# Normalised input moved from MID to H, squares in a four-slot buffer, and a new order of the token tiles in one feed-forward stage

## The reference

```python
xc = jnp.concatenate([o1, o2], axis=-1) @ up_w + up_b     # (2048, 512) @ (512, 1024)
x = residual + xc                                         # residual = xn
h = rmsnorm(x, norm2_w)                                   # x * rsqrt(mean(x*x) + 1e-6) * w
ffn = jax.nn.gelu(h @ ffn_w1 + ffn_b1, approximate=False) @ ffn_w2 + ffn_b2
return x + ffn                                            # hidden size 2048
```

## Time and profile before

| | us |
|---|---|
| median of 2 runs | 2920.51 (2918.38 to 2922.63) |
| profiled execution, its own time | 2919.8 |
| span of its slowest core (core 2) | 2918.3 |
| spans of the eight cores | 2908.5 to 2918.3 |
| TensorE busy, of the span | 2542.4 (87%) |
| VectorE busy, ScalarE busy | 559.1 (19%), 627.8 (22%) |

### The profile page before, as it was taken

The page is one execution under the profiler, slowest core; times in us unless marked ns, Lnnn a source line. Parts: engine busy times, 40 slices in busy tenths (PEclk is TensorE's granted clock), DMA queues, the critical chain, the costliest instruction groups (busy, mean ns, idle before and its releaser), DMA issues.

```text
span 2918.3 us, 30150 instructions; the slowest of 8 cores (2908.5 to 2918.3 us)
## 1 busy us (share of the span) xinstructions
PE 2542.4 (87%) x11144; PEld 1120.6 (38%) x11344; DVE 559.1 (19%) x699; ACT 627.8 (22%) x966; POOL 61.6 (2%) x80
## 2 busy tenths in 40 slices
PE   3865665666896978999999999999999999999999
PEld 1322332332332433444444444444444444444443
DVE  5115743643214000010011001001100100100000
ACT  2332232330111211112211211221121122112222
POOL 0000000000000010000000000000000000000000
PEclk9986555556896989999999999999999999999999
DMA  6020000007000047007007007007006105203011
GB/s 148 15 46 1 1 1 1 1 1 116 1 0 1 1 62 112 1 1 116 1 1 116 1 1 116 0 1 102 14 1 90 26 1 74 42 1 58 33 41 44
DMA packets 65621, 100.92 MB, mean 35 GB/s; under 512 B 4819, under 2 KB 40148, under 8 KB 65484
## 3 DMA queue, kind: packets, MB, share of 16 engines
q0 software_dynamic: 58080, 80.78, 19.1%
q1 hardware_dynamic: 7404, 18.20, 1.9%
HBM read 171.36 MB, written 8.39 MB: 62 GB/s over the span
## 4 chain that ended last, share of the span: by engine, by line
PE 85%; issue 7%; DVE 4%; DMA 2%; ACT 2%; SPq 0%; another core or an unknown queue 0%; POOL 0%; DVEq 0%; ACTq 0%; POOLq 0%
PE PF L1119 31%; PE PF L1100 29%; PE PF L1008 4%; PE PF L983 4%; PE PBF L682 3%; PE PF L697 3%; PE PF L381 2%; DMA WE<-e2w 1%; PE PBF L925 1%; PE PF L639 1%; PE PF L556 1%; PE PBF L341 1%; DVE H L972 1%; DMA c_qb<-qb 1%; PE PF L712 1%
## 5 line engine op out<-in xcount | busy, mean ns | idle before, releaser
L1119 PE MATMUL PF<-WE,EHS 128*128 128x512 bf16 x4016 | 913.5, 380 | 34.1 <-DMA WE<-e2w 10.0
L1100 PE MATMUL PF<-XN,WE 128*128 128x512 bf16 x4012 | 887.3, 380 | 19.1 <-DMA WE<-e1w 14.7
L1107 ACT ACTIVATE EHS<-PF,c_eb1c 128x512 bf16<-128x512 f32 x512 | 352.2, 688 | 1348.1 <-PE PF L1100 1346.0
L1119 PEld LDWEIGHTS PF<-WE,EHS 128*128 128x128 bf16 x4096 | 390.5, 98 | 544.8 <-issue 100.9
L1100 PEld LDWEIGHTS PF<-XN,WE 128*128 128x128 bf16 x4096 | 401.3, 98 | 499.8 <-issue 20.4
L1137 DVE SCALAR_TENSOR_TENSOR S<-PF,WTM,S 128x1024 bf16<-128x1024 f32 x128 | 164.3, 1284 | 1688.5 <-PE PF L1119 1469.5
L682 PE MATMUL PBF<-c_idb,E 120*120 120x120 bf16 (+1 forms) x288 | 91.2, 317 | 52.7 <-DVE E L676 15.1
L983 PE MATMUL PF<-H,WF 128*128 128x512 bf16 x502 | 119.2, 399 | 8.0 <-ACT MID L990 7.0
L1008 PE MATMUL PF<-WF,MID 128*128 128x512 bf16 x500 | 115.4, 380 | 4.6 <-ACT MID L990 3.9
L697 PE MATMUL PF<-PTS,VT 120*32 120x120 bf16 x272 | 70.9, 261 | 36.5 <-ACT UPIN L722 1.1
L682 PEld LDWEIGHTS PBF<-c_idb,E 120*120 120x120 bf16 (+1 forms) x288 | 48.8, 169 | 92.9 <-issue 90.7
(11 more groups left out here) (129 smaller groups left out, 970.7 us busy)
## 6 DMA issues: line engine op xcount, KB each, us to landing
WE<-e1w POOLq DMA_DIRECT2D x32, 1024.0 KB, 41.4
WE<-e2w POOLq DMA_DIRECT2D x32, 1024.0 KB, 20.7
XST<-x SPq DMA_DIRECT2D x16, 512.0 KB, 3.4
out<-OST SPq DMA_DIRECT2D x16, 512.0 KB, 2.6
WF<-f1w POOLq DMA_DIRECT2D x1, 4096.0 KB, 29.1
WF<-f2w POOLq DMA_DIRECT2D x1, 4096.0 KB, 53.9
WR<-r1w POOLq DMA_DIRECT2D x1, 2048.0 KB, 31.5
WDOWN<-dw POOLq DMA_DIRECT2D x1, 1024.0 KB, 18.8
```

Source lines behind the costliest of these rows:

```text
L1100: (lambda m=m, nt=nt, k=k, ps=ps, slot=slot: t_.matmul(ps[:, 0:512], WE13[slot][:, k, 128 * m: 128 * m + 128], XN3[:, k, 512 * nt: 512 * n ...
L1107: P.op("scalar", (lambda e=e, m=m, ps=ps: s_.activation(EHS3[:, m, 0:512], ps[:, 0:512], AF.Silu, bias=CS["eb1c"][:, 16 * e + m: 16 * e + ...
L1119: lambda k=k, h2=h2, tcl=tcl, e=e, PEx=PEx: t_.matmul(PEx[0:128, 512 * h2: 512 * h2 + 512], EHS3[:, k, 128 * tcl: 128 * tcl + 128], WE23[: ...
```

## The change

`XA` moves from the two halves of `MID` into the half of `H` that the tile's normalised values will take, so `a4_h` works in place, and `XA`'s resource is that half's. Squares go to the first 2048 columns of `MID`, which hold four of them: `a4_sq` now records four squares, their four statistics matmuls, four squares, four matmuls, and `a4_stats` keeps only Ln and Exp. The order by hand is new: tiles 0 and 1 pass one after the other through up, transposes, squares and statistics; of tile 2, up and transposes stand before the second feed-forward matmul of tile 1 and the rest after it; tile 3 follows with all its steps. No operation is added or removed and no transfer changes.

```diff
             wload(WF2[:, :].rearrange("p (k m) -> p k m", k=16),
                   CN["f2w"].ap().rearrange("(k p) m -> p k m", p=128), rWF2, "dwf2")
             MID3 = MID[:, :].rearrange("p (c x) -> p c x", c=16)
-            XA3L = [MID3[:, 8:16, :], MID3[:, 0:8, :]]
-            rXAL = [rMID, rMID]
             H3 = H[:, :].rearrange("p (c x) -> p c x", c=8)
+            XA3L = [H3[:, :, 0:512], H3[:, :, 512:1024]]
+            rXAL = rH
+            SQM = MID[:, 0: 4 * 512]
             pbanks = [(PA, rPA), (PB, rPB)]
 
             def a4_up(nt):
@@ -937,19 +938,20 @@
                 hs = nt % 2
                 XA3 = XA3L[hs]
                 for c in range(8):
-                    sq = H3[:, c, 512 * (1 - hs): 512 * (1 - hs) + 512]
+                    sq = SQM[:, 512 * (c % 4): 512 * (c % 4) + 512]
                     P.op("vector", (lambda c=c, sq=sq, XA3=XA3: v_.tensor_tensor(
                         sq, XA3[:, c, 0:512], XA3[:, c, 0:512], ALU.mult)),
-                        rd=[rXAL[hs]], wr=[rH[1 - hs]])
+                        rd=[rXAL[hs]], wr=[rMID])
+                    if c % 4 == 3:
+                        for cc in range(c - 3, c + 1):
+                            sq2 = SQM[:, 512 * (cc % 4): 512 * (cc % 4) + 512]
+                            P.op("tensor", (lambda cc=cc, sq2=sq2: t_.matmul(
+                                PS[0:1, 0:512], CS["onesb"][:, 0:1], sq2,
+                                start=(cc == 0), stop=(cc == 7))),
+                                rd=[rMID, rCS["onesb"]], wr=[rPS])
 
             def a4_stats(nt):
                 hs = nt % 2
-                for c in range(8):
-                    sq = H3[:, c, 512 * (1 - hs): 512 * (1 - hs) + 512]
-                    P.op("tensor", (lambda c=c, sq=sq: t_.matmul(
-                        PS[0:1, 0:512], CS["onesb"][:, 0:1], sq,
-                        start=(c == 0), stop=(c == 7))),
-                        rd=[rH[1 - hs], rCS["onesb"]], wr=[rPS])
                 P.op("scalar", (lambda hs=hs: s_.activation(
                     RST2[0:1, 512 * hs: 512 * hs + 512], PS[0:1, 0:512], AF.Ln,
                     bias=CS["epsc"][0:1, 1:2], scale=1.0 / 1024)),
@@ -1034,22 +1036,34 @@
                                      ALU.add)),
                                 rd=[rph], wr=[rS[tc]])
 
-            for pr in range(2):
-                n0, n1 = 2 * pr, 2 * pr + 1
-                a4_up(n0)
-                a4_up(n1)
-                a4_sq(n0)
-                a4_trans(n0)
-                a4_stats(n0)
-                a4_sq(n1)
-                a4_trans(n1)
-                a4_stats(n1)
-                a4_h(n0)
-                a4_h(n1)
-                a4_ffn1(n0)
-                a4_ffn2(n0)
-                a4_ffn1(n1)
-                a4_ffn2(n1)
+            def a4_pass1(nt):
+                a4_up(nt)
+                a4_trans(nt)
+                a4_sq(nt)
+                a4_stats(nt)
+
+            a4_pass1(0)
+            a4_pass1(1)
+            a4_h(0)
+            a4_h(1)
+            a4_ffn1(0)
+            a4_ffn2(0)
+            a4_ffn1(1)
+            a4_up(2)
+            a4_trans(2)
+            a4_ffn2(1)
+            a4_sq(2)
+            a4_stats(2)
+            a4_h(2)
+            a4_up(3)
+            a4_trans(3)
+            a4_sq(3)
+            a4_stats(3)
+            a4_h(3)
+            a4_ffn1(2)
+            a4_ffn2(2)
+            a4_ffn1(3)
+            a4_ffn2(3)
             P.fence()
             P.replay(blk)
         esA4.close()
```

## The result

| | before | after |
|---|---|---|
| median of all executions, us | 2922.01 (12) | 2938.04 (13) |
| profiled execution's slowest core, us | 2918.3 | 2935.5 |
| ratio to before, 95% interval | | 1.0068 (1.0044 to 1.0092) |
| `a4_up`(0) to the last ffn2, core 2, us | 388.8 | 405.4 |
| the same, median of the eight cores, us | 385.9 | 404.6 |

In some executions of both kernels one die ran at a lower clock; the comparisons here leave these out, with medians of 2920.2 us before and 2937.4 us after (8 executions each), except that the ratio, one of means, still holds one such execution of 2963.89 us. So the kernel became 17.2 us or 0.6% slower, in these medians as in the two profiled executions. Of the 17.2 us between the profiled ones, 16.6 lie in the changed stage and 0.7 behind it. On the median of the eight cores the stage grew by 18.7.

A forecast was written before the change was run, and what follows sets the result against it. TensorE was taken as the bound, 85% of the chain that ended last, plus its waits. Terms −10.7 + 12.6 + 14.9 = +16.8 us on the profiled execution gave 2936.6 us; range 2931 to 2943, to hold 8 in 10.

The forecast's parts named there:

- up(3): Tile 3's `a4_up`, its evictions queued behind tile 2's multiplies on VectorE: 9.1 us, bounds 7.8 and 12.
- ffn2(1): Tile 1's second feed-forward matmul starts cold behind tile 2's transposes: 31.0 us plus 2.3 lost.
- Part 2: First prologue, one tile at a time: up, transposes, squares and statistics in series, 33.1 us per tile; cost +12.6 us.
- Part 3: Start of ffn1(1) to start of ffn1(2): interleaving tile 2 takes 141.3 instead of 126.4 us; cost +14.9 us.
- Tile 2's statistics: After ffn2(1), from tile 2's first statistics matmul to its last: 6.8 us.
- Ln with its table load: Tile 2's Ln after its statistics, with a table load no transposes cover: 2.33 + 1.28 = 3.6 us.
- Part 1: First ffn1 of each pair: moving XA out of MID frees the first Gelu; gain 4.7 + 6.0 = 10.7 us.
- The clock falls again: Inside each pair's first ffn1, a shorter pause still drops the clock; 1.6 + 3.2 us return, 2941; chance 0.13.
- The clock stays up in the prologues: Prologues avoid the half clock, worth 20.7 us together, so 2916 and not slower; chance 0.04.
- The squares hide: Statistics' waits for squares total 20.8 us; if half of them vanished, 2926; chance 0.03.
- The Gelu stall stays: First Gelu still held, now by statistics reading `MID`: 2947, 10.7 above the forecast; chance 0.04.

The follow-up runs named there:

- the third experiment: Changed kernel with eight slots for squares and, for tiles 0, 1 and 3, squares recorded ahead of the transposes; 2923.9 us, ratio 1.002.
- e9: Old order with new layout, grouped transposes and statistics, early `a4_h`; then squares on ScalarE, sixteen slots, another statistics PSUM bank, new order: 2842.5 us, ratio 0.9756.

## Why the prediction was right

- **Range and sign.** 2936.6 was forecast; the medians went from 2920.2 to 2937.4. That is 17.2 us, with 16.8 in the sum. The waits lie where they were said to be: two groups of statistics with 2.33 us between them and 2.87 behind the transposes, 4.42 us before up(3)'s third group, a clock of 0.92 in ffn2(1).
- **Part 2, first pair.** +12.6 forecast; +11.2 on core 2 (79.2 against 68.0) and +11.8 on the median. The two gaps are 2.87 and 2.33 us where the working has 2.95 from the transposes' end and 2.26. On core 2 the difference is the clock: I let the second `a4_up` start as cold as the first, but from 705 on its granted clock was 1.00, 1.2 us after its start at 703.77, and it took 9.65 us, not 10.85, to the transposes.
- **Part 3, second pair.** +14.9 forecast; +16.6 on core 2, +15.1 on the median. On core 2 ffn2(1) lost 2.34 us (forecast 2.3), but on the median only 1.3. Up(3) was the least certain term: on core 2 it took 10.1 us from the end of the multiplies at 917.2 to 927.3, not 9.1, inside its bounds of 7.8 to 12. Tile 2's statistics took 7.3 us from the first to the start of the last and not 6.8: they stepped by 0.735 throughout. Ln with its table load came as priced: 904.66 to 908.27 is 3.61.
- **Part 1, the layout.** 10.7 forecast; 11.2 on core 2, but 8.0 on the median (35.8 to 31.2 and 34.5 to 31.1). This is the term that was mis-sized, and its reason was taken from one core. The working reads a second fall of the clock off core 2 in both ffn1 and puts it down to the stall. On the eight cores of the kernel before, ffn1(0) has that fall on six and ffn1(2) on two, though the stall stands on all. Core 4 stood longer than core 2's 3.14 us and kept its clock:

```profile
937.65 22.61 PE L983 MATMUL PF<-H,WF 128*128 128x512 bf16 x102 [3.71 <-ACT MID L990]
```
```profile
928.82:962.91 34.09, 29.35 (x125) 12.72 (x127) 5.79 (x8) 12.28 (x17) 0.00 (x0) 0.95 0.00 0
```

Without the fall a first ffn1 took 34.1 to 34.5 us, so the stall alone is worth 3.4; with it, 35.6 to 37.1. The new length, 31.1, was right within 0.3 us.
- **That the sum came so close is partly luck.** On core 2 the errors were −1.4, +1.7 and −0.5 us, together −0.2 in the stage. On the medians the parts are −8.0, +11.8 and +15.1, and the stage grew by 18.7, 1.9 more than forecast; the forecast started from core 2, whose stage was the longest of the eight before (388.8 us) by 1.7 us. The 0.7 us behind the stage is not explained; on the eight cores that part is 1856.5 to 1860.0 before and 1856.6 to 1860.0 after, so I take it for scatter.
- **The rivals.** *The clock falls again* inside ffn1: it did so on none of the eight cores; after the cold start both first ffn1 stayed at 1.00. *The clock stays up in the prologues*: 0.63 and 0.61, no. *The squares hide*: they don't, and the third experiment shows that they could. *The Gelu stall stays*: 0.43 us are left. The table load of 1.28 us was all that a switch cost here: it starts 3.33 us after ffn1(0)'s first matmul, as the first group of eight ends, and from its start at 752.64 to the end of two Gelus 2.82 us pass. That leaves no room for the drain of 1.38 us that the Trainium skill ("ScalarE: Activation LUTs", section "What ACT_TABLE_LOAD costs") adds.

What the prediction did not see is what else was to be had: it called the Gelu wait the change's "one useful thing" and overlooked the wait of tile 0's transposes for tile 1's evictions, and it took the steps of transposes and statistics as given. The larger cost in both kernels was the 0.31 us by which each transpose waited for the last, and the steps of 0.36 and 0.41 us were in the earlier trace rows all along.

## What to carry to other kernels

When a buffer is moved and the order is changed in one edit, price them apart: here the first gains about 10 us and the second loses 29. An order by hand gained here where it put work of *different* engines side by side; moving TensorE's work earlier in TensorE's own queue hid nothing, and what then stands behind other work on an in-order engine (squares behind adds, evictions behind multiplies) is what the next engine waits for. Look also at the step between equal small instructions: if it is several times what their columns need, see whether they wait for one another; here one operation for the lot was worth 32 to 46 us, more than any reordering alone brought. And take the length of a step from all cores before a sum rests on it.

## What the runs showed of the hardware

- Cores that ran the same program differed in when the granted clock rose and whether it fell again. The first pair's two `a4_up` of the kernel before took 19.3 to 20.2 us over the eight cores and ffn1(2) 34.1 to 37.1, with a clock of 0.95 on core 4 and 0.85 on core 2. Steps that began at full clock, like its ffn1(1), agreed within 0.01 us.
- Transposes recorded in groups of eight ran 0.066 us apart at a granted clock of 1.00 and 0.117 at 0.50, and the eight statistics matmuls of tile 0 in e9 0.236 us apart at 1.00. With a wait between each two, transposes stepped 0.36 to 0.41 us and statistics 0.735, and the clock was at 0.50 for the greater part of them (0.64 over tile 2's transposes after the change). The window from 689.46 to 693.48 of e9, core 4, holds 32 transposes, a broadcast and TensorE's waits:

```profile
689.46:693.48 4.02, 3.24 (x35) 2.10 (x33) 3.46 (x6) 1.26 (x2) 0.00 (x0) 1.00 1.02 172
```
- ScalarE squared 128x512 in 0.63 us beside VectorE's evictions without slowing them: eight evictions still came 1.05 us apart.
